# Expert rows scattered into token order instead of gathered back, in a fused attention and mixture-of-experts kernel

## The reference, cut to what matters

```
xn = layernorm(x)
s  = attention(xn): layernorm again, low-rank q, k, v (128), 16 heads of 64, rotary, softmax, w_out, + xn
g  = silu(experts(xn))
experts: logits = xn @ router_w.T; top 2 of 8 experts per token, weights normalized
         rank of each (token, choice) pair within its expert; pairs with rank >= 2561 are dropped
         out_buf[e, slot] = silu(buf @ w1[e]) @ w2[e]
         combined[token] = sum over the 2 choices of weight * out_buf[their slot];  + xn
result = x + s * g
```

## Time and profile before

| | us |
|---|---|
| runs | 3955.34, 3968.85, 3965.55 |
| median | 3965.55 |
| the profiled execution, its own time | 3965.41 |
| its span, first to last instruction | 3963.7 |
| granted TensorE clock, mean | 0.975 of full speed |
| projection | 0 to 280 |
| routing | 282 to 317 |
| attention | 318 to 2873 |
| experts | 2875 to 3720 |
| combination | 3720 to 3964 |

### The profile page before, as it was taken

How to read it: one execution, slowest core, us unless ns; L and a number is a source line. 1 busy time by engine, 2 the same in 40 slices (tenths; PEclk the granted TensorE clock), 3 DMA queues, 4 the chain that set the end, 5 groups by cost and what they waited for, 6 DMA issues and landing times. The chain is left out here.

```text
span 3963.7 us, 77467 instructions
## 1 busy us (share of the span) xinstructions
PE 3761.8 (95%) x24384; PEld 2382.4 (60%) x24384; DVE 3361.8 (85%) x4562; ACT 2807.9 (71%) x4042; POOL 800.7 (20%) x714
## 2 busy tenths in 40 slices
PE   6974999999999999999999999999789999999887
PEld 4652444444444444444444444444389999999887
DVE  5436999999999999999999999999677778787787
ACT  3433788787878787878878787887566667667554
POOL 1103444400000000000000000000044444444487
PEclk9886999999999999999999999999999999999999
DMA  6753344444444444444444444444166666666786
GB/s 240 267 219 103 102 138 126 138 124 129 132 121 132 121 138 120 144 122 133 131 122 132 121 133 122 141 122 118 45 237 228 219 227 223 228 223 227 248 294 219
DMA packets 384687, 644.92 MB, mean 163 GB/s; under 512 B 138800, under 2 KB 271664, under 8 KB 348528
## 3 DMA queue, kind: packets, MB, share of 16 engines
q1 hardware_dynamic: 342896, 450.83, 36.6%
q0 software_dynamic: 39680, 192.78, 14.5%
q10 hardware_dynamic: 2048, 0.53, 0.1%
HBM read 453.27 MB, written 122.04 MB: 145 GB/s over the span
## 5 line engine op out<-in xcount | busy, mean ns | idle before, releaser
L841 ACT ACTIVATE at_ex<-at_st 128x1024 f32<-128x1024 f32 x1024 | 1046.9, 1023 | 120.9 <-PE at_st L966 98.8
L979 PE MATMUL at_pv<-at_ex,at_v 128*64 128x512 f32 x4096 | 991.5, 605 | 0.0
L864 ACT ACTIVATE at_fr<-at_fr 128x512 f32<-128x512 f32 x1024 | 599.6, 586 | 340.0 <-PE at_fr L989 288.8
L721 DVE TENSOR_REDUCE at_mx<-at_fr 128x1 f32<-128x512 f32 x1024 | 703.3, 687 | 137.0 <-PE at_fr L986 80.1
L1214 POOL DMA_INDIRECT seam_stage<-in_w,keep_widx x142 | 184.7, 1300 | 2498.5 <-POOLq L481 2077.1
L732 DVE TENSOR_TENSOR at_sum<-at_sum,at_ex 128x1024 f32<-128x1024 f32 x512 | 624.8, 1220 | 13.8 <-ACT at_ex L841 2.3
L979 PEld LDWEIGHTS at_pv<-at_ex,at_v 128*64 128x64 f32 x4096 | 248.4, 136 | 508.3 <-issue 493.0
L989 PE MATMUL at_fr<-at_kfar,at_qh 64*128 64x512 f32 x1024 | 467.3, 456 | 15.6 <-DVE at_mx L721 6.1
L986 PE MATMUL at_fr<-at_kdif,at_qh 64*128 64x512 f32 x1024 | 472.2, 461 | 4.7 <-DVE at_mx L721 4.7
L986 PEld LDWEIGHTS at_fr<-at_kdif,at_qh 64*128 64x128 f32 x1024 | 188.8, 184 | 419.1 <-issue 407.9
L1364 PE MATMUL ex_o<-ex_w,ex_hT 128*128 128x256 f32 x3408 | 417.5, 282 | 0.0
(11 more groups left out here) (157 smaller groups left out, 5597.9 us busy)
## 6 DMA issues: line engine op xcount, KB each, us to landing
at_cq<-scr_c SPq DMA_DIRECT2D x62, 1024.0 KB
at_ck<-scr_c SPq DMA_DIRECT2D x62, 1024.0 KB
scr_v<-pj_v SPq DMA_DIRECT2D x64, 512.0 KB, 4.5
at_v<-scr_v SPq DMA_DIRECT2D x64, 512.0 KB
at_swpq<-at_rawq SPq DMA_DIRECT2D x128, 256.0 KB
at_swpk<-at_rawk SPq DMA_DIRECT2D x128, 256.0 KB
at_rec<-scr_rec SPq DMA_DIRECT2D x256, 128.0 KB
scr_o<-at_oT SPq DMA_DIRECT2D x64, 512.0 KB
```

Of the source, the lines that this page charges most:

```text
L721: e.reduce_max(mx[k // QB][:, h * QB + k % QB:h * QB + k % QB + 1], fr[h][:, :], AX.X).then_inc(s_tr[h], 1)
L841: e.activation(ex[k][:, :, :], st[u % 2][:, :, :], ACT.Exp, scale=SCALE).then_inc(s_exp, 1)
L864: e.activation(fr[h][:, :], fr[h][:, :], ACT.Relu).then_inc(s_pos[h], 1)
L979: mm = e.matmul(pv[n][rows[h], :], v[i.u][:, kt, rows[h]], ex[kt][:, h, :], start=(kt == 0), stop=(kt == KT - 1))
```

## The change

- Experts: SP no longer stores `ex_out`. POOL scatters each group's result by two indirect DMAs (L1232) whose row numbers stand in `slots`, into `scr_eo`, now in the order token, choice. It does so four groups late (`LAG`), ahead of the next w1 gather, and the last four behind the loop. Slots without a pair carry a number beyond the bounds and are skipped.
- The table now holds token times 2 plus choice, so DVE computes the token's number from it with three small operations ahead of the first group.
- Attention: POOL also writes zeros over `scr_eo` (64 DMAs of 256 KiB, one for each tile), since no group writes the rows of dropped pairs.
- Routing: `read` and its two operations per choice are gone.
- Combination: no gathers. SP loads `scr_eo` plainly, 2 MiB for each batch in one DMA.
- Projection: POOL loads batch 1 of x, and SP the constants `wvraw` and `wraw`, only once batch 0 of x has landed; DVE no longer waits for the constants. PE does the router's matmuls of batch 0 between turning xn and turning h.

```
 # project_phase
+            e.dma_start(lnp[:, :, :], io["lnp"]).then_inc(s_const, 16)
+            e.wait_ge(s_x[0], 16)
             e.dma_start(wvraw[:, :], io["wvT"]).then_inc(s_const, 16)
-            e.dma_start(lnp[:, :, :], io["lnp"]).then_inc(s_const, 16)
             e.dma_start(wraw[:, :, :, :], io["wqk"].rearrange("r d w p -> d r w p")).then_inc(s_pw, 16)
...
-            for u in range(2):
-                load(At(0, u))
+            load(At(0, 0))
+            e.wait_ge(s_x[0], 16)
+            load(At(0, 1))
...
             e.sem_inc(s_lgd, 1)
-            e.wait_ge(s_const, NCONST)
...
+            def batch(a, first):
+                turn(a, xn[a.u], XNT, 4)
+                if first:
+                    router(a)
+                turn(a, h, HT, 8)
+                if not first:
+                    router(a)
 # route_phase
-                then(e.tensor_scalar(rk[:, :], rk[:, :], float(CAP - 1), None, ALU.min))
-                then(e.tensor_tensor(out=keep["read"][:, :, k], in0=rk[:, :], in1=pos[:, :], op=ALU.add))
 # attend_phase, GpSimd, once for each of 64 tiles
+                e.dma_start(scr["eo"].rearrange("(i p n) d -> i p (n d)", i=NPAIR, p=P)[i.n(), :, :], zeros[:, :]).then_inc(s_blanked, 16)
 # experts_phase, SyncE
-            def store(a):
-                e.wait_ge(s_oe, a.n(1, 1))
-                e.dma_start(scr["eo"].rearrange("(g c p) d -> g p c d", c=GT, p=P)[a.n(), :, :, :], out[a.u][:, :, :]).then_inc(s_os[a.u], 16)
 # experts_phase, GpSimd
+            def scatter(g):
+                e.wait_ge(s_oe, g + 1)
+                for c in range(GT):
+                    e.indirect_dma_start(out=scr["eo"], out_offset=bass.IndirectOffsetOnAxis(ap=slots[:, g * GT + c:g * GT + c + 1], axis=0),
+                                         in_=out[g % 2][:, c, :], in_offset=None, bounds_check=2 * NTOK - 1, oob_is_err=False).then_inc(s_os[g % 2], 16)
             for g in range(GROUPS):
                 q = g % 2
+                if g >= LAG:
+                    scatter(g - LAG)
...
+            for g in range(GROUPS - LAG, GROUPS):
+                scatter(g)
 # combine_phase, SyncE
+            def load_eo(a):
+                e.dma_start(eo[a.u][:, :, :, :].rearrange("p t k d -> p t (k d)"),
+                            scr["eo"].rearrange("(b t p k) d -> b p t (k d)", t=TB, p=P, k=2)[a.n(), :, :, :]).then_inc(s_eo[a.u], 16)
...
                 store(a)
                 if after:
                     load_x(a.next(2))
+                    load_eo(a.next(2))
...
+            load_eo(At(0, 0))
             load_o(At(0, 0), 1)
-            e.wait_ge(s_g[0], 32)
+            e.wait_ge(s_ol, CT)
             load_x(At(0, 1))
-            e.wait_ge(s_ol, CT)
             load_o(At(0, 1), 0)
+            load_eo(At(0, 1))
 # combine_phase, GpSimd
-            for n in range(NT):
-                if n >= NG:
-                    e.wait_ge(s_mix, 2 * (n - NG + 1))
-                for j in range(2):
-                    e.indirect_dma_start(out=eo[n % NG][j][:, :], out_offset=None, in_=scr["eo"],
-                                         in_offset=bass.IndirectOffsetOnAxis(ap=keep["read"][:, n, j:j + 1], axis=0)).then_inc(s_g[n % NG], 16)
```

More of the change, by code:

```diff
@@ L305, in _ @@
             e.wait_ge(s_const, NCONST)
[L306 to L323, removed]
-                    for t in range(TB):
[L325 to L345, removed]
@@ new lines, in turn, with fill, router @@
+            def turn(a, src, k0, ready):
+                e.wait_ge(s_ln, a.n(8, ready))
+                for k in range(KD):
+                    out = fill(a, k0 + k)
+                    for t in range(TB):
+                        mm = e.transpose(out[:, t * P:(t + 1) * P], src[:, t, k * P:(k + 1) * P], keep["ident"][:, :])
+                    mm.then_inc(s_pa, 1)
+            def fill(a, k):
+                e.wait_ge(s_act, a.n(ITEMS, k + 1))
+                return pa[k % 2]
+            def router(a):
+                e.wait_ge(s_act, emptied(a, XNT + 1))
+                e.wait_ge(s_lgd, a.n(1, 1))
+                for t in range(TB):
+                    for k in range(KD):
+                        mm = e.matmul(lg[:, t, :], xnT[:, k, t * P:(t + 1) * P], rw[:, k, :], start=(k == 0), stop=(k == KD - 1))
+                mm.then_inc(s_lgf, 1)
@@ L348, in route_phase @@
+            batch(At(0, 0), True)
+            with e.Fori(0, NBATCH // 2 - 1) as it:
+                for off in (1, 2):
+                    batch(At(it, off), False)
+            batch(At(0, NBATCH - 1), False)
 def route_phase(nc, io, scr, keep):
@@ L1187, in _ @@
             e.dma_start(slots[:, :], scr["table"].rearrange("(p n) o -> p (n o)", p=P)).then_inc(s_slots, 16)
-            def store(a):
-                e.wait_ge(s_oe, a.n(1, 1))
-                e.dma_start(scr["eo"].rearrange("(g c p) d -> g p c d", c=GT, p=P)[a.n(), :, :, :], out[a.u][:, :, :]).then_inc(s_os[a.u], 16)
-            for q in range(2):
-                e.sem_inc(s_os[q], 16)
-            groups(e, store)
             e.wait_ge(s_w2l, 2 * (GROUPS - 1))
@@ L1204, in _ @@
                         io["x"][0, :, :].rearrange("(t p) d -> p t d", p=P)).then_inc(seam["x"], 16)
-            store(At(0, GROUPS - 1))
             e.wait_ge(seam["o"], 16)
             e.wait_ge(seam["x"], 16)
-            for q in range(2):
-                e.wait_ge(s_os[q], 16 * ((GROUPS - q + 1) // 2 + 1))
         @blk.gpsimd
@@ L1231, in _ @@
                 weights(g, io["w2"], raw2[q], s_w2[q])
+            for g in range(GROUPS - LAG, GROUPS):
+                scatter(g)
+            for q in range(2):
+                e.wait_ge(s_os[q], 16 * GT * ((GROUPS - q + 1) // 2))
         @blk.vector
@@ L1255, in outputs @@
             def outputs(a):
-                e.wait_ge(s_os[a.u], a.same(16, 16))
+                wait(e, s_os[a.u], a.same(16 * GT))
                 e.wait_ge(s_o, a.n(1, 1))
@@ L1270, in body @@
                 low2(one, 1)
+            e.wait_ge(s_slots, 16)
+            e.tensor_scalar(half[:, :], slots[:, :], float(2 * NTOK - 1), 0.5, ALU.min, ALU.mult).then_inc(s_rows, 1)
+            e.wait_ge(s_rows, 1)
+            e.tensor_scalar(half[:, :], half[:, :], -0.25, WHOLE, ALU.add, ALU.add).then_inc(s_rows, 1)
+            e.wait_ge(s_rows, 2)
+            e.tensor_scalar(rows[:, :], half[:, :], -WHOLE, None, ALU.add).then_inc(s_rows, 1)
             low1(At(0, 0), 0)
@@ L1408, in combine_phase @@
         s_ld = [seam["x"], sem("ld1")]
-        s_g = [sem(f"rows{k}") for k in range(NG)]
+        s_eo = [sem(f"eo{u}") for u in range(2)]
         s_st = [sem(f"st{u}") for u in range(2)]
@@ L1483, in tile @@
                 e.wait_ge(s_mix, a.n(2 * TB, 2 * t + 1))
-                e.scalar_tensor_tensor(out=mix[k][:, :], in0=eo[t % NG][1][:, :], scalar=g2[u][:, t, 1:2], in1=mix[k][:, :], op0=ALU.mult, op1=ALU.add).then_inc(s_mix, 1)
+                e.scalar_tensor_tensor(out=mix[k][:, :], in0=eo[u][:, t, 1, :], scalar=g2[u][:, t, 1:2], in1=mix[k][:, :], op0=ALU.mult, op1=ALU.add).then_inc(s_mix, 1)
                 if back:
@@ L1505, in batch @@
                 e.wait_ge(s_st[a.u], a.same(16, 16))
+                e.wait_ge(s_eo[a.u], a.same(16, 16))
                 e.wait_ge(s_g2, a.n(1, 1))
```

65 lines of the change are left out of this document (43 added, 22 removed).

## The result

| | before | after |
|---|---|---|
| median of 9 runs each, us | 3959.18 (3952.02 to 3968.85) | 3946.07 (3938.80 to 3948.91) |
| the profiled execution, its own time | 3965.41 | 3946.07 |
| its span | 3963.7 | 3944.5 |
| granted TensorE clock, mean | 0.975 | 0.975 |

The ratio of after to before is 0.9959, with a 95% interval of 0.9946 to 0.9973: 16.2 us faster (10.7 to 21.4). That is the difference of the means of the nine runs; the medians differ by 13.1. The forecast was 12.8 us faster, 3952.6, with a range of 3935 to 3965. It started from 3965.4, which the nine runs of before do not bear out: their median is 3959.18.

The account below looks back on a forecast made before the run. TensorE was taken to bound attention and experts, GpSimd's gathers nearly all of the combination. Terms -9.2 -3.3 +3.4 -1.6 +0.9 +1.8 +0.7 -1.0 -4.5 gave -12.8: 3965.4 to 3952.6 us, range 3935 to 3965.

Parts of the forecast that it names:

- Steady state: Combination, six intervals between stores: batches of 27.1 us against 28.7, -9.2 us in all.
- The hold: Combination: DVE, then TensorE, held 3.5 us a batch because half 1 of the attention output lands late.
- Rivals A and B: Combination: A, half 1 (nearly) in time, 3931 to 3942, chance 0.17; B, batches stay about 28.7 us, 3962, chance 0.22.
- Last interval: Combination, from store 6 to the last store: nothing left to load, about 21.8 us against 25.2, -3.3 us.
- Combination's start: First tile +3.4 us later behind the experts' rows; the rest up to store 0 -1.6 us.
- 0 in the middle: Experts' phase: two added scatters a group fit into GpSimd's 6.1 us rest, costing 0.
- Rival C: Experts: long scatters delay w1, TensorE waits every group, from 8.6 us for two; 3993 at 4.3 each; chance 0.06.
- The start: Experts' phase: three small DVE operations between the table's landing and the first token gather, +0.9 us (0 to 1.3).
- The end: Experts' phase: last two scatters and their landing before the next phase's first load, +1.8 us (1.2 to 4).
- Attention: Zero writes can meet only the phase's first loads, +0.7 us (0 to 4); over 4 us longer means wrong.
- Routing: Two operations, done twice, go away: -1.0 us.
- Projection: DVE needs only batch 0 of x and starts earlier: -4.5 us (-2.5 to -6.5).

Follow-up runs that it names:

- rows_behind: after, with the combination's loop loading the next batch's experts' rows behind half 1 of the attention output instead of ahead: 3918.42 us, 0.9886 of before.
- rows_half_2: after, loading only half of the experts' rows in the combination (tiles 0 to 3, reused for 4 to 7): 3983.95 us, one execution, batches 24.6 us.
- no_blank: after without the 64 DMAs that write zeros over scr_eo in attention: 3939.28 us, 0.9937 of before.
- old_proj: after with the projection phase of before: 3948.21 us, 0.9979 of before.
- before_again: before, unchanged, run for a second profile: 3953.31 us.
- scatter_x3: after with every scatter of the experts' result done three times, six a group, the extra ones into unread scratch tensors: 4163.91 us.
- best: after with experts' rows loaded behind half 1, in the loop and at the start, and zeros written behind the last table scatter: 3918.72 us, 0.9903 of before.
- proj_only: before with the projection phase of after, nothing else: 3950.16 us, 0.9973 of before.
- one_zero_2: after with a single 256 KiB DMA of zeros behind the last table scatter instead of 64: 4006.30 us, one execution.
- router_back_2: after with the router's matmuls of batch 0 again behind the turning of h: 4009.11 us, one execution.

## Why the prediction came out right

**Steady state: right in mechanism and size.** -9.2 was forecast and -9.0 measured in the two profiles (27.2 against 28.7). Half 1 was to land 21.9 us behind a batch's start. It was used at 3804.57, 21.3 us behind the one at 3785.19 - 1.9; over the six batches this is 21.3 to 22.8 us, 21.9 in the mean. The hold was to be 3.5 us and is 3.7 (27.2 against the 23.5 of rows_behind); rows_half_2 takes 2.6 of the forecast 3.0 off it. Only the length of before's batches was a matter of the execution: they were 29.4 and 29.5 us in two other profiles, and by these the gain is 13 us. The Trainium skill, "DMA: Bandwidth & Descriptors", section "Anatomy of one DMA", would have had the half in time, at 18.3 us, by its 436 GB/s, which it states for a DMA issued from GpSimd. These loads are from SP, and the trace does not agree: 21.9 us. Rivals A and B both fell.

**Last interval: mis-sized.** -3.3 forecast, -5.9 measured: 19.63 - 0.40 = 19.2 us between the last stores against 25.2. I had counted seven tiles and a bit at 2.96 us. But DVE has no more splits to do in the last batch from its third tile on, and catches up with TensorE; two of its tiles took 1.92 us each:

```profile
3924.30 0.42 DVE L1504 TENSOR_TENSOR cb_att<-cb_pj,cb_xn 128x256 f32<-128x256 f32 x1
...
3926.22 0.42 DVE L1504 TENSOR_TENSOR cb_att<-cb_pj,cb_xn 128x256 f32<-128x256 f32 x1
...
3928.14 0.42 DVE L1504 TENSOR_TENSOR cb_att<-cb_pj,cb_xn 128x256 f32<-128x256 f32 x1
```

The size is partly the execution's too: in six other profiles with this combination the interval is 20.6 to 21.5 us (25.0 to 25.9 in the three with gathers), -4.9 by the means. The granted clock from the hold of batch 6 to the end is 0.94 in after, 0.85 in no_blank and 0.83 in old_proj.

**Combination's start: right together.** The first tile came 4.3 us later (3.4 forecast), the rest up to store 0 was 3.0 shorter (1.6 forecast): +1.3 against +1.8.

**Experts: 0 in the middle was right, its limit was wrong.** The 7.2 us in the two profiles are the execution's; against before_again the middle is 1.3 us longer. GpSimd's rest in a group fell from 6.1 us to 3.1, as forecast. Rival C's point, 8.6 us, added the time from landing to use to GpSimd's rest. That reserve can be spent once; in every group only the rest of 6.1 us can count, and scatter_x3, with 7.8 us, bears this out. C was not near on this count: the two scatters took 2.6 us. But a slower experts' phase did come, on one chip, by a way that no rival named. The start cost 0.1 (0.9 forecast). The end cost 3.3 us (1.8 forecast, 4 at most): from the last copy to the next phase 6.85 us against 3.54. SP's and POOL's rows there:

```profile
3709.23 0.97 POOL L1232 DMA_INDIRECT scr_eo<-ex_out,ex_slots  x1 [7.32 <-DVE ex_out L1282]
3710.50 0.97 POOL L1232 DMA_INDIRECT scr_eo<-ex_out,ex_slots  x1 [0.30 <-issue]
```

```profile
3714.59 0.37 SPq L1456 DMA_DIRECT2D cb_eo<-scr_eo  x1
```

From the end of the second issue to the next phase's first load 3.1 us pass.

**Attention: the step that failed.** "Only the phase's first loads can be met by one of them: +0.7 (0 to 4)". It is +5.8 by the means and 6.2 in the two profiles, over the 4 us that the prediction named as a sign of being wrong. 3.4 us of it lie in the phase's tail, about 2000 us behind the last zeros, where each of the last four waits for a 4 KB store is 1 us longer or more; why is open.

**Routing** -1.0, as forecast. **Projection** -4.5 forecast; -4.4 are the change's at the start, -6.7 the difference of the means, which the clock's spread of 11 us makes unsure. The router's move gave nothing, as forecast.

By the means of the table (the experts without the slow chip) the parts are -6.7 projection, -1.0 routing, +5.8 attention, +1.6 experts, -15.7 combination: -16.0, against 16.2 measured. The prediction's -12.8 came that close by luck: attention's 5.1 us too many stood against a combination, a projection and an experts' phase that came out 5.0, 2.2 and 1.1 us better than forecast.

Two sums of the prediction do not come out. The ends of its terms add up to 3948 to 3964, not to 3946 to 3960. And two scatters of 1.23 us make 3.1 us only with two gaps of 0.3 us and not one.

## What to carry to other kernels

In one queue the place of a load matters as much as its size: what is needed next batch goes behind what is needed in this one. Here that gave 22 us for two moved lines, more than the whole change. A stage difference between two single profiles of under 10 us is not an effect until a second profile of the same code shows it. The same code gave 832.8 and 841.3 us for the experts' middle, and 265.4 to 276.3 for the projection. And count on no more than an engine's idle time per turn of a loop; what a buffer gives on top is spent once. That everything below it is free isn't shown, and on one chip it was not.

## What the runs showed of the hardware

- With 16.8 MB of zeros written early in a phase, the last four of its 128 waits for the landing of a 4 KB store took 2.7 to 3.4 us instead of 1.6 to 2.1, some 1800 to 2000 us later (the last zeros were issued at 1044 us in best and 820 in after, the tail begins near 2820); with 256 KiB they did not. The cause is open.
- With several MiB issued on SP's queue and not landed, the issue itself takes long: 1.28 and 2.15 us for the loads of `cb_eo` and `cb_raw` above, 0.37 for the phase's first.
- The same block of 48 matmuls takes 5.6 or 5.8 us, in a pattern that differs between executions of one program; the experts' middle differed by 8.5 us between two such executions (841.3 and 832.8).
- The 12 times of proj_only lie between 3940 and 3970 us and before's 17 beside them between 3955 and 3975, those of after between 3939 and 3949, those of old_proj between 3942 and 3959. The kernels with gathers vary more; in which stage is not known.
- One chip ran the changed experts' phase 63 us longer: there one_zero_2 and router_back_2 took 4006 and 4009 us and before 3953, one execution each, so the change would very likely lose there. A change of 0.4% should be timed on more than one chip.
